# Second attention of a two-layer model: probabilities split in fp16 as the stationary operand, and a new order of its steps

## The reference, cut to what matters

```
xn, ln = layernorm(context), layernorm(layernorm(x))
q  = (ln @ Wq)                        # 16 heads x 64
k, v = concat([xn @ Wkv, ln @ Wkv])   # 512 rows
sim = rmsnorm(q, qn_g) / 8 @ rmsnorm(k, kn_g).T   # masked by key
attn = softmax(sim)
x = x + (attn @ v) @ Wout + bout
```

## Time and profile before

| | |
|---|---|
| median of 3 runs | 1427.76 us (1427.2 to 1428.42) |
| the profiled execution | 1431.85 us, its span 1430.1 us |
| granted TensorE clock, mean | 0.899 |
| busy: PE, DVE, ACT, POOL | 1083.9, 1062.6, 791.4, 439.7 us |
| attention of layer 1 | 536 to 1262 us of the span |

### The profile page before, as it was taken

How to read it: one execution, slowest core, us unless ns; L and a number is a source line. 1 busy time by engine, 2 the same in 40 slices (tenths; PEclk the granted TensorE clock), 3 DMA queues, 4 the chain that set the end, 5 groups by cost and what they waited for, 6 DMA issues and landing times. The chain is left out here.

```text
span 1430.1 us, 23649 instructions
## 1 busy us (share of the span) xinstructions
PE 1083.9 (76%) x7410; PEld 706.4 (49%) x7410; DVE 1062.6 (74%) x1847; ACT 791.4 (55%) x1340; POOL 439.7 (31%) x410
## 2 busy tenths in 40 slices
PE   1388888438999314889989898998999989936746
PEld 0245555314444202557656565666666656723435
DVE  8478898685666686787888878888878888657941
ACT  2237777524555224776876677766777677632122
POOL 7010000115777305332233322333312333010135
PEclk9689999668999656999999999999999999978968
DMA  4302110100000200000000000000000000050040
GB/s 183 86 8 25 14 23 1 33 3 17 22 22 11 92 0 1 1 1 1 1 1 0 0 0 0 0 0 0 0 0 0 0 0 1 1 202 1 21 130 25
DMA packets 22587, 33.22 MB, mean 23 GB/s; under 512 B 3856, under 2 KB 19711, under 8 KB 21446
## 3 DMA queue, kind: packets, MB, share of 16 engines
q1 hardware_dynamic: 21096, 29.74, 7.2%
q0 software_dynamic: 1440, 2.82, 0.6%
HBM read 26.52 MB, written 8.77 MB: 25 GB/s over the span
## 5 line engine op out<-in xcount | busy, mean ns | idle before, releaser
L1430 PE MATMUL e_mix<-e_probs,e_v_ones 128*128 128x256 f32 x1024 | 280.8, 393 | 3.8 <-ACT e_mixed L1499 2.4
L1291 POOL TENSOR_TENSOR e_raw<-e_raw,e_inv 128x512 f32<-128x512 f32 x96 | 115.8, 1214 | 387.7 <-DVE e_inv L1557 387.7
L1430 PEld LDWEIGHTS e_mix<-e_probs,e_v_ones 128*128 128x128 f32 x1024 | 179.7, 194 | 45.4 <-issue 25.2
L1574 DVE TENSOR_REDUCE e_row_max<-e_row_scores 128x1 f32<-128x512 f32 x256 | 165.7, 680 | 16.3 <-PE e_row_scores L1359 15.9
L1522 ACT ACTIVATE e_probs<-e_scores 128x512 f32<-128x512 f32 x256 | 142.4, 598 | 25.8 <-PE e_scores L1418 24.4
L1299 POOL TENSOR_TENSOR e_natural<-e_raw,e_natural 128x512 f16<-128x512 f32 x96 | 114.7, 1194 | 59.2 <-DVE e_natural L1568 59.2
L1359 PE MATMUL e_row_scores<-e_k_high,e_q_high 65*128 65x512 f16 x256 | 90.3, 387 | 55.8 <-DVE e_row_max L1574 50.7
L1418 PE MATMUL e_scores<-e_q_high,e_k_high 128*128 128x256 f16 x512 | 130.0, 286 | 0.0
L1417 PE MATMUL e_scores<-e_q_stack,e_k_stack 128*128 128x256 f16 x512 | 129.3, 285 | 0.0
L1614 DVE RECIPROCAL e_inverse<-e_summed 128x256 f32<-128x256 f32 x64 | 111.7, 1746 | 7.4 <-ACT e_mixed L1499 7.2
L1542 DVE TENSOR_REDUCE e_sum_sq<-e_squares 128x8 f32<-128x512 f32 x96 | 65.7, 685 | 62.5 <-ACT e_squares L1470 61.2
(11 more groups left out here) (361 smaller groups left out, 2583.1 us busy)
## 6 DMA issues: line engine op xcount, KB each, us to landing
w<-in_w SPq DMA_DIRECT2D x2, 2048.0 KB, 9.9
c_w<-in_w SPq DMA_DIRECT2D x17, 192.0 KB, 2.4
placed_scratch<-in_no_rows SPq DMA_DIRECT2D x1, 2313.0 KB, 17.0
a_mask_q<-in_mask_q SPq DMA_DIRECT2D x1, 2048.0 KB, 10.3
a_mask_k<-in_mask_k SPq DMA_DIRECT2D x1, 2048.0 KB, 14.7
parts_scratch<-a_parts SPq DMA_DIRECT2D x2, 1024.0 KB, 4.0
k_stack<-parts_scratch SPq DMA_DIRECT2D x24, 64.0 KB
q_stack<-parts_scratch SPq DMA_DIRECT2D x24, 64.0 KB
```

The lines of the kernel that those rows point to most:

```text
L1291: nc.gpsimd.tensor_tensor(raw[:, j], raw[:, j], bc(inv[:, HU * j:HU * j + HU], (P, HU, D1), 2), ALU.mult).then_inc(normed, 1)
L1430: mm = pe.matmul(mix[:, 0:S], v_ones[par][:, kt, h, :], probs[buf][:, kt, :], start=(kt == 0), stop=(kt == KT - 1))
L1574: dve.tensor_reduce(row_max[:, i, qt:qt + 1], row_scores[qt][:], AX.X, ALU.max).then_inc(max_done, 1)
```

## The change

Only `attend_layer1` and its tables and planner are written anew:

- `s`: all four key tiles of a head into one double bank (`scores[i]`), and two exponentials of it on ACT, each 128x1024: `probs` in f32 and `p_hi` in f16. The low part `p_lo` is their difference: for the first head on DVE in the same step (`lo` 0), for the second on POOL in the next step (`lo` 1).
- `w`: the probabilities are the stationary operand. A head is 24 matmuls with 64 or 65 moving columns: high with V high (and a column of ones), high with V low, low with V high. V is split into f16 parts by ACT (copy) and DVE (`low_values`). Both heads of the pair before are done in a step, after this step's first scores.
- `n`: DVE takes the reciprocal of 128x4 and multiplies straight from PSUM. `a`: PE turns `attended` back (two f32 transposes), ACT copies it.
- `r`: maxima two pairs ahead, with the sign turned by the reduction itself, and one bank in place of two. `m`: one f32 transpose, a copy of 4x128 on ACT, and a DMA by SP to the row of `q_high`.
- `k_high` and `q_high` are filled by DMA (SP) in place of DVE.
- `raw` has two buffers, and a unit's `k`, `q`, `root` and first two tiles are prepared two units ahead. `norm`, `hi` and `low` of a tile are events of their own. Before the first step the program now also prepares all of unit 1's raws, its root and two tiles, and the maxima of two pairs.

```diff
-JOBS = [[("q", t) for t in range(QT)] + [("v", t) for t in range(3)],
...
-SPLITS = [[("root",)], [("split", j) for j in range(4)], [("split", j) for j in range(4, 6)], []]
+KQ = [("k", t) for t in range(KT)] + [("q", t) for t in range(QT)]
+RAWS = [KQ[0:2], KQ[2:3], KQ[3:6], []]
+SPLITS = [[2, 3], [4, 5], [], [0, 1]]
+TURNS = [[("tk", 0), ("tk", 1)], [("tk", 2), ("tk", 3), ("tq", 0), ("tq", 1)], [], []]
+VALUES = [[], [], [0], [1, 2, 3]]
+ROWS_AHEAD = 2
...
+    jobs = [("o",)] if s == 2 and not first else []
+    jobs += [("a",)] if not (first and s < 2) else []
...
+    jobs += turns[:2] + raws + values + turns[2:] + [None] * 8
...
+    if p != 2:
+        out = norm0 + s0 + r[0] + lo1 + job[0] + hi0 + w[0] + r[1] + job[1] + lo0 + low0 + s1 + r[2] + norm1 + job[2] \
+            + w[1] + hi1 + r[3] + job[3] + n + low1 + m + job[4]
     else:
...
+        out = s0 + lo1 + job[0] + job[1] + w[0] + r[0] + job[2] + s1 + r[1] + lo0 + job[3] + w[1] + r[2] + job[4] + n + r[3] + m
+    out += job[5] + job[6] + job[7]
+    if p == 2 and there(2):
+        out.append(("root", 2))
     return out
...
+START = unit_start(0, 6) + [("tk", t, 0) for t in range(KT)] + [("tq", t, 0) for t in range(QT)]
+for _q in range(ROWS_AHEAD):
+    START += [("r", i, qt, _q) for i in range(2) for qt in range(QT)] + [("m", _q)]
+START += unit_start(1, 2)
...
+            def copy_high(event, use, par):
...
+                    dma = sp.dma_start(k_high[par][0:D1, :, cols], k_stack[par][0:D1, :, cols])
...
+            def low_probs(q, buf, i):
+                pool.wait_ge(exp_done, 2 * (2 * q + i + 1))
+                nc.gpsimd.tensor_tensor(p_lo[buf][i][:], probs[i][:], p_hi[buf][i][:], ALU.subtract).then_inc(lo_done[i], 1)
...
+            def weigh(q, i, par, p):
+                buf = p % 2
+                pe.wait_ge(lo_done[i], q + 1)
+                if not (isinstance(q, int) and q == 0):
+
+                    pe.wait_ge(att_done, q)
+                h = 2 * p + i
+                for qt in range(QT):
+                    at = slice(P * qt, P * qt + P)
+                    out = mix[:, i, (D1 + 1) * qt:(D1 + 1) * (qt + 1)]
+                    for kt in range(KT):
+                        values = v_cols[par][:, kt, h, :]
+                        first, last = qt == 0 and kt == 0, kt == KT - 1
+                        pe.matmul(out, p_hi[buf][i][:, kt, at], values[:, 0:D1 + 1], start=first, stop=False, skip_group_check=True)
+                        pe.matmul(out[:, 0:D1], p_hi[buf][i][:, kt, at], values[:, D1 + 1:2 * D1 + 1], start=False, stop=False, skip_group_check=True)
+                        mm = pe.matmul(out, p_lo[buf][i][:, kt, at], values[:, 0:D1 + 1], start=False, stop=last, skip_group_check=True)
+                mm.then_inc(weighed, 1)
```

More of the change, by code:

```diff
@@ L1082 @@
+SPLITS = [[2, 3], [4, 5], [], [0, 1]]
+TURNS = [[("tk", 0), ("tk", 1)], [("tk", 2), ("tk", 3), ("tq", 0), ("tq", 1)], [], []]
+VALUES = [[], [], [0], [1, 2, 3]]
+ROWS_AHEAD = 2
 NEWTON = 3
 RSQRT_BITS = float(0x5f3759df)
-M_AT = 2
+VC1 = 2 * D1 + 2
 def plan_step(s, first, last):
[L1094 to L1106, removed]
-    else:
[L1108 to L1120, removed]
-    return out
@@ L1124, with there @@
[L1124 to L1127, removed]
+    hf, p = divmod(s, PU)
+    def there(du):
+        return not (last and hf + du >= 2)
+    ahead, behind = not (last and s + ROWS_AHEAD >= 2 * PU), not (first and s == 0)
@@ new lines, in plan_step, with unit_start @@
+    out += job[5] + job[6] + job[7]
+    if p == 2 and there(2):
+        out.append(("root", 2))
+    return out
+MISC = ("k", "q", "v", "tk", "tq", "o", "m", "a")
+def unit_start(u, splits):
+    out = [(name, t, u) for name, t in KQ] + [("root", u)]
+    for j in range(splits):
+        out += [("norm", j, u)] + ([("v", j, u)] if u == 0 and j < KT else []) + [("hi", j, u), ("low", j, u)]
+    return out
+START = unit_start(0, 6) + [("tk", t, 0) for t in range(KT)] + [("tq", t, 0) for t in range(QT)]
@@ L1222, in attend_layer1 @@
         probs = [sb(f"probs{i}", [P, KT, S], F32) for i in range(2)]
[L1223 to L1232, removed]
-        scores = [psum(f"scores{i}", [P, 2, S]) for i in range(3)]
@@ new lines, in batch @@
+            def batch(bt):
+                b = bt.b
+                for s, events, _ in bt.steps():
+                    hf, p = s // PU, s % PU
+                    if p == 0 and not (bt.last and hf):
+                        if not (bt.first and hf == 0):
+                            sp.wait_ge(scored, HU * (UB * b + hf))
+                        masks(b + hf, 1 - hf)
+                    for event, use in events:
+                        if event[0] in ("tk", "tq"):
+                            copy_high(event, use, 1 - hf)
+                        elif event[0] == "m":
+                            place_max(use, hf if p + ROWS_AHEAD < PU else 1 - hf, (p + ROWS_AHEAD) % PU)
@@ new lines, in turn_max, with rows @@
+                pe.transpose(bank[0:2 * QT, 0:P], neg_max[buf][:], ident32[:]).then_inc(ready, 1)
+            def rows(q, par, p, i, qt):
+                n = 4 * q + 2 * i + qt
+                if not (isinstance(n, int) and n == 0):
+                    pe.wait_ge(max_done, n)
+                h = 2 * p + i
+                pe.matmul(row_scores[:], q_high[par][0:MASK1 + 1, h, P * qt:P * qt + P], k_high[par][0:MASK1 + 1, h, :],
+                          start=True, stop=True).then_inc(rows_ready, 1)
@@ L1414, in batch @@
[L1414 to L1418 removed]
+                            if i == 0:
+                                pe.wait_ge(max_in[p % 2], 16 * (PU * b + s // 2 + 1))
@@ new lines, in batch @@
+                            if not (bt.first and s == 0):
+                                pe.wait_ge(exp_done, 2 * (2 * q + i - 1))
+                            for kt in range(KT):
+                                out = scores[i][:, kt, :]
+                                cols = slice(P * kt, P * kt + P)
+                                pe.matmul(out, k_stack[hf][:, h, cols], q_stack[hf][:, h, :], start=(kt % 2 == 0), stop=False, skip_group_check=True)
+                                mm = pe.matmul(out, k_high[hf][:, h, cols], q_high[hf][:, h, :], start=False, stop=True, skip_group_check=True)
```

553 lines of the change are left out of this document (282 added, 271 removed).

## The result

The changed kernel took 1479.87 us (median of 4 runs, 1471.4 to 1492.49) against 1427.48 (4 runs): ratio 1.0374, with an interval from 1.0286 to 1.0462. Slower, as forecast.

What follows compares the result with a forecast made beforehand. It took the second attention to be bound by four engine queues in fixed order that wait for each other. Terms of +20.8, +19.9 and -8.0 gave +32.7 us: 1464.5 for the profiled execution, 1460 against the median, range 1397 to 1494.

Steps and rivals of the forecast that it cites:

- Its own case: Whole kernel: slower, at 1435 to 1480 us, with a chance of 0.42.
- the shared port: Second attention: a DVE cast stands still until POOL's running instruction, here a 2.3 us split, is over.
- The walk: Step-by-step timing of a unit (four head pairs, half a batch): 44.5 us, 45.3 on average with the output projection.
- third step longest (near 14): Sign of being right: a unit's third step is its longest, with DVE idle before k3's sum of squares.
- The third step: Third step of a unit: DVE idles 4.5 us until ACT serves k3 after s0's exponentials; 14.8 us including root.
- The rival with 56 ns: Weight loads bound the new f16 products on PE at 56 ns each: +36 us, 1496 us, chance 0.07.
- The copies by DMA, hidden: Copies to k_high and q_high land in 2.6 us; up to about 3.9 us cost nothing, 4.9 adds 1 a unit.
- Start: Preparation before the second attention's first step: tiles no longer overlap, maxima go through one bank; +20.8 us.
- Fourteen full units: Second attention's main part: 634.4 us against 614.5, so +19.9 us.
- The last two units and the tail: End of the second attention: steps without preparation are short, 60.6 us against 68.6, so -8.0 us.
- The clock: Rival: PE's granted clock falls to 0.85, adding 4.4 us a unit, half on the path; +31, 1491 us, chance 0.17.
- The sums win: Rival: port waits are short, a unit takes some 4.2 us less, kernel faster at 1401 us, chance 0.30.

Runs made afterwards that it cites:

- a1: The changed kernel with GpSimd's low split of the second head's probabilities on only one of four key tiles: 1459.66 us, ratio 1.0158.
- a3: The changed kernel with the third step reordered, k3's projection leading and the second head's scores ahead of the first row scores: 1496.81 us, ratio 1.0444.
- a4: The changed kernel without the product of the probabilities' high half with the values' low half, 16 products a head instead of 24: 1478.45 us, ratio 1.0301.
- e1: The changed kernel with the two query copies a unit on VectorE instead of by DMA, key copies still by DMA: 1499.37 us, ratio 1.046.
- d1: The kernel before with only the six copies a unit of the turned high halves issued as DMAs: 1450.92 us, ratio 1.0135.
- c1_start: The changed kernel with unit 1's six projections put one by one between the first two pairs' row maxima in the start: 1477.97 us, ratio 1.0348.
- d3: The kernel before with the high-half copies by DMA and ScalarE's copies of turned tiles as fp32 words: 1428.59 us, ratio 0.9966.
- d4: The kernel before with ScalarE's copies as fp32 words, key copies by DMA and the two query copies on VectorE: 1393.86 us, ratio 0.9732.

## Why the prediction was right, point by point

The forecast was slower, 1460 us, with a range from 1397 to 1494; measured 1479.87. Its own case, 1435 to 1480, just holds it. The units grew for a reason that it gave, the shared port; that the sum came so near is in part luck, as its terms show.

- *The unit.* The walk gave 45.3 us. Measured 45.1 without the gaps at the jump, 45.7 with them. Its steps, from scaling to scaling: third 11.35 against 11.2 to 11.9, fourth 13.2 against 12.7, first and second together 19.9 against 18.5 (the walk gives no scaling for the first; its 11.5 us end with the sum of squares of k1). The projection was 2.4 in each second unit; it measured 4.4, since both the third and the fourth step grow. So a unit without it was put 1.7 too long (44.5 against 42.8) and one with it 0.3 too short (46.9 against 47.2): the average is better than its terms. The sign "third step longest (near 14)" holds only if the root is counted in: 15.8 us from the second step's reciprocal, at 841.28, to the root's end. From reciprocal to reciprocal the fourth step is the longest.
- *The shared port.* "A DVE cast ... stands still until POOL's running instruction is over": 2.33 us behind a split of 2.13 (forecast 2.3), 0.3 after its end; a1 shows the cost, 2 us a unit. But the casts' mean was 0.86 us and not 1.5, because in the first and second steps only some of them meet the split. And the sum of 7.2 us a pair against 8.9 compares unlike things: it has each cast alone, at 0.35, while casts of 0.76 are in the 8.9 (640 to 1140 us).
- *The third step.* VectorE idled 5.57 us before k3's sum of squares (forecast 4.5), and the step's length was right. That the sum of squares is what holds the step was wrong: a3 moved the idle time without taking it away.
- *The products.* In the changed kernel 24 of them follow each other from 866.99 to 867.72 us, 30 ns each; the forecast was 28. The rival with 56 ns fell. a4 shows that they do not bound the stage; I had put half of any surplus on the path.
- *The copies by DMA, hidden: "up to about 3.9 us cost nothing".* They landed in 2.6 as taken, and TensorE waited 7.7 us for them in all; e1 agrees. In the order of before the same DMAs are not hidden: 40.5 us of waits in d1.
- *The sum, part by part,* each from one row maximum (r0) to another. Start: +20.8 forecast, +15.8 measured. Fourteen full units: +19.9 forecast; from r0 of the first step to r0 of the 57th it takes 636.6 us against 607.6, +29.0, of which 8.2 are the two gaps at the jump. The last two units and the tail: -8.0 forecast, 71.8 us against 75.0, -3.2. So the start was 5.0 too dear and the tail 4.8 too cheap, which is luck, and the units without the gaps came out at +20.8 beside 19.9. (The walk took 614.5 us for fourteen units of before, up to a mark at 1194; between like marks it is 607.6.)
- *What was missing: the gap at the jump.* No step of the prediction had it, and nothing in the trace of before shows it. Two gaps, 8 us, in the profiled run; by the profile of e1 up to five, 23 us. Without it the profiled execution would have been near 1465, beside the sum's 1464.5. The median of 1479.9 lies where three or four gaps would put it, but only the profiled run's two were seen.
- *The clock.* As a rival it was to fall to 0.85 and cost 31 us. It fell to 0.93 in the window from 640 to 1140 us (before 0.97). What it costs can be read from steps of one kind, which differ by little else: third step with the projection 12.6 at 1.00 and 14.2 at 0.89, second step 9.5 and 10.2 at 0.83; before, fourth step 9.97 at 1.00 and 11.36 at 0.95. With each kind at its shortest a unit would take 44.4 us instead of 45.1, and 42.8 instead of 43.7 in the kernel before. So by this count the lower clock takes 0.7 to 0.8 us a unit in both, and the 1.4 between them is not the clock's. The fourth step without the projection limits it: it ran at 0.87 in every unit of the changed kernel, so its length at 1.00 is not known.
- *"The sums win"* fell: the busy sums shrank and no time came of it. VectorE was priced at 7.2 us a pair, 58 in a batch; it has 66.9 in the batch at 822.82 against 70.9 before, and 8.5 of them are casts and splits that stand still. ScalarE, priced as unchanged at 8.0 a pair, fell to 7.3.

What stays open: the 1.4 us by which a unit is longer without the gaps are less than the 2 that GpSimd's split costs (a1 is at 43.1, below the 43.7 of before), so the split covers them by size; yet the f32 products, the large reciprocal and the mix copies that left should have bought more than that. That they show as no more than 0.6 us a unit, even with the split shortened, is seen; that TensorE's single bank for row scores (it waits 100.2 us for maxima now) is the reason was not tried.

## What to carry to other kernels

Where no engine is full, less work is no gain by itself: name for each removed piece the wait that ends with it. A large change may hold small parts that gain: here two of them alone, fp32 words in ScalarE's copies and the key copies by DMA with the queries' kept on VectorE, gave 2.7% in the old order, while the whole change is 3.7% slower. A copy goes to DMA where it has slack, and stays on an engine where it is the last thing before its reader.

## What was not expected of the hardware

- Behind the jump back of a loop that had grown on TensorE from 508 to 756 recorded matmuls a lap, TensorE stood for 3.3 to 5.1 us in some laps, with nine more instruction packets of 16.4 KB for each such gap. It came in none to all of five laps: two in the changed kernel, none in c1_start, which has the same loop, five in e1. So the none of a4 (626) does not show that a shorter loop is free of it.
- With a third of the products gone the granted clock was lower (0.89 instead of 0.93 from 640 to 1140 us, 0.67 in one step), and the unit took 45.4 us instead of 45.1.
- GpSimd's 2.13 us instruction held a cast of 0.41 us for 2.33; cut to 0.67 us, it gave back 2 us a unit.
- Two copies of 0.42 us a unit, taken back from a DMA of 2.6 us to VectorE, changed the whole kernel by 2.3% (d3 against d4).
